# Edge passes of a graph network: row tiles in a ring, a resident table of node blocks, and edge sums in two column halves

## The reference

```
def gatv2_layer(x, src, dst, Wl, Wr, att, bias, n_nodes, heads):
    xl = (x @ Wl).reshape(N, heads, Dh)
    xr = (x @ Wr).reshape(N, heads, Dh)
    e = leaky_relu(xl[src] + xr[dst], 0.2)
    logits = einsum('ehd,hd->eh', e, att)
    m = segment_max(logits, dst)
    a = exp(logits - m[dst])
    alpha = a / segment_sum(a, dst)[dst]
    out = segment_sum(alpha[:, :, None] * xl[src], dst)
    return out.mean(axis=1) + bias

h = relu(gatv2_layer(x, ..., heads=8)); h = gatv2_layer(h, ..., heads=4)   # with a loop edge per node
x = layernorm(x + h)
agg = segment_sum(x[src], dst)
x = layernorm(x + dense3(x + agg))
```

## Time and profile before

| | us |
|---|---|
| median of 3 runs | 4044.32 |
| lowest, highest | 4044.29, 4049.66 |
| span of the profiled execution | 4048.7 |

### The profile page before, as it was taken

How to read it: one execution, slowest core, us unless ns; L and a number is a source line. 1 busy time by engine, 2 the same in 40 slices (tenths; PEclk the granted TensorE clock), 3 DMA queues, 4 the chain that set the end, 5 groups by cost and what they waited for, 6 DMA issues and landing times. The chain is left out here.

```text
span 4048.7 us, 76266 instructions
## 1 busy us (share of the span) xinstructions
PE 3293.6 (81%) x24199; PEld 2204.4 (54%) x24199; DVE 2807.3 (69%) x6887; ACT 1717.6 (42%) x3696; POOL 2796.9 (69%) x2157
## 2 busy tenths in 40 slices
PE   0399999999999999996339977777777777568986
PEld 0246666666666666674226655554455555346763
DVE  3558888888888888886537755565555555579972
ACT  3254444444444444432215433333333333147861
POOL 4488888888777777505678888888888885537630
PEclk9999999999999999986669988888888888569997
DMA  2233343343333333323114433333333332211210
GB/s 58 51 65 80 86 88 86 86 89 85 80 87 86 86 85 88 75 54 83 48 36 79 91 74 67 68 69 67 67 68 73 69 68 48 52 26 40 44 34 28
DMA packets 607173, 274.68 MB, mean 68 GB/s; under 512 B 445801, under 2 KB 568077, under 8 KB 606260
## 3 DMA queue, kind: packets, MB, share of 16 engines
q1 hardware_dynamic: 261848, 102.14, 11.7%
q0 software_dynamic: 107328, 77.78, 11.1%
q10 hardware_dynamic: 237600, 89.88, 9.1%
HBM read 161.25 MB, written 105.94 MB: 66 GB/s over the span
## 5 line engine op out<-in xcount | busy, mean ns | idle before, releaser
L901 PE MATMUL L_e_ps_z<-L_e_xT,L_w_abs 128*128 128x500 f32 x2700 | 1501.4, 642 | 0.0
L826 POOL DMA_INDIRECT L_e_xs<-in_x_dram,src_idx x880 | 1193.1, 1356 | 335.4 <-issue 261.4
L826 POOL DMA_INDIRECT L_e_xs<-x_d,src_idx x820 | 1079.7, 1317 | 253.3 <-issue 249.8
L952 PEld LDWEIGHTS L_e_ps_v<-L_e_xs,L_e_p 125*128 125x128 f32 x5400 | 860.0, 204 | 628.3 <-issue 569.6
L996 ACT ACTIVATE L_e_rl<-L_e_ps_z 128x500 f32<-128x500 f32 x1350 | 793.0, 587 | 883.0 <-PE L_e_ps_z L901 883.0
L952 PE MATMUL L_e_ps_v<-L_e_xs,L_e_p 125*128 125x65 f32 x5400 | 796.2, 274 | 11.1 <-DVE L_e_acc L1180 9.4
L1180 DVE SCALAR_TENSOR_TENSOR L_e_acc<-L_e_acc,L_e_row,L_e_ps_v 128x130 f32<-128x130 f32 (+1 forms) x1440 | 448.5, 311 | 424.1 <-PE L_e_ps_v L952 281.4
L888 PE MATMUL L_e_ps_x<-ident,L_e_xs 125*64 125x125 f32 x1800 | 288.7, 285 | 310.7 <-DMA L_e_xs<-x_d,src_idx 251.8
L989 ACT ACTIVATE L_e_xT<-L_e_ps_x 128x500 f32<-128x500 f32 x450 | 264.3, 587 | 619.3 <-PE L_e_ps_x L891 590.4
L901 PEld LDWEIGHTS L_e_ps_z<-L_e_xT,L_w_abs 128*128 128x128 f32 x2700 | 427.4, 198 | 77.8 <-issue 24.3
L1163 DVE TENSOR_TENSOR L_e_p<-L_e_ohc,L_e_ae 125x640 f32<-125x640 f32 x540 | 427.1, 818 | 0.0
(11 more groups left out here) (304 smaller groups left out, 3620.2 us busy)
## 6 DMA issues: line engine op xcount, KB each, us to landing
L_v_d<-L_e_acc ACTq DMA_DIRECT2D x225, 260.0 KB
L_e_dlb<-dloc_d SPq DMA_DIRECT2D x90, 468.8 KB, 4.9
L_v_d<-L_e_acc ACTq DMA_DIRECT2D x225, 130.0 KB
L_e_xw<-x_d SPq DMA_DIRECT2D x1800, 12.0 KB
L_e_xs<-in_x_dram,src_idx POOLq DMA_INDIRECT x900
L_e_xs<-x_d,src_idx POOLq DMA_INDIRECT x900
L_e_lim<-limits_d SPq DMA_DIRECT2D x180, 39.1 KB
L_max_d<-L_e_me SPq DMA_DIRECT2D x45, 78.1 KB
```

Of the source, the lines that this page charges most:

```text
L826: pool.indirect_dma_start(xs[c.slot(XR)][:, n, 0:D], None, lay.x_rows, bass.IndirectOffsetOnAxis(k.src_idx[:, u:u + 1], 0)).then_inc(gath[ ...
L901: pe.matmul(ps_z[part % ZR][:, 0:QT], lay.w_abs[:, part * 128:(part + 1) * 128], xT[q][:], start=True, stop=True).then_inc(s["z_ready"], 1)
L952: ins = pe.matmul(ps_v[u // 2 % 2][:, u % 2 * VX + v * XW:u % 2 * VX + (v + 1) * XW], p[st % 3][:, u % NQ, v, :, :].rearrange("e n h -> e ...
```

## The change

It does four things.

1. **Tiles instead of units are gathered.** `src_tile` holds the row numbers of the 800 tiles. GpSimd gathers tiles in fetches of 16 (`TF`) into a ring of 64 tiles (`TR`), `e_tiles`. For a fetch it waits for a count (`copied`) that says that the chunks which use the old tiles have been copied, and it signals a fetch that has landed (`fetched_to`) when four gathers of the next are issued. For each chunk SP waits for the fetch that it needs and then copies its 20 tiles from the ring into `xs` with 20 SBUF-to-SBUF DMAs at places from registers (`load_rows`). `xs` is a ring of 6 chunks in both layers. In layer 1 two fetches are made in the block before the pass and one chunk is served there; in layer 2 two fetches in each of the two blocks, and chunks 0, 1, 2 served.
2. **The windows are resident.** All 98 window blocks are loaded once a layer (`lay.xw`, 96 rows, 64 zero columns ahead of them). `turn` takes 128 columns of it from a place in a register as the stationary side, so that the product fills all of `ps_x`; the transposes come after it and overwrite the upper half. The places are loaded on TensorE at the end of the step before (`window_blocks`).
3. **Each sum is two products of 64 columns**, the one to PSUM partitions 0 to 63, the other to 64 to 127. The sums of a quad stand together, after `turn`, and the projection parts together behind them.
4. **Setup**: 2 of the 9 source gathers by unit remain (the neighbour sum uses them), tiles are turned with 8 transposes, and three lists of units (place of the window, place in the ring, fetch needed) are stored in `unit_d`. In layer 1 the rings of `dlb` and of the limits have two slots instead of three, and one `p` buffer lies in memory of a later tensor. The copy of `dlb` for a chunk is still queued on SP behind the loads for that chunk.

```
-AHEAD = (1, 4)
-EARLY = 35
+TR = 64
+TF = 16
+NF = G // TF
+RF = TR // TF
+XR = 6
+LR = 8
+SERVED = (1, 3)
+FETCHED = (2, 4)
...
+def counts(eng, name, places):
+    regs = [eng.alloc_register(f"{name}{n}") for n in range(places.shape[1])]
+    eng.load(regs, places)
+    return [(eng.snap(r, donate=True, min_val=0, max_val=63) & 63) + 1 for r in regs]
+
+def fetch_tiles(k, pool, lay, f0, f1):
+    for f in range(f0, f1):
+        if f >= RF:
+            if (f - RF) % 16 == 0:
+                copies = counts(pool, f"{lay.nm}reuse{f}_", k.reuse[0:1, f - RF:min(f + 16, f1) - RF])
+            pool.wait_ge(lay.copied, copies[(f - RF) % 16])
+            pool.sem_inc(lay.freed, 1)
+        for i in range(TF):
+            g = f * TF + i
+            pool.indirect_dma_start(lay.tiles[:, g % TR * D:(g % TR + 1) * D], None, lay.x_rows,
+                                    bass.IndirectOffsetOnAxis(k.src_tile[:, g:g + 1], 0)).then_inc(lay.gath[f % RF], 16)
+            if i == 3 and f > f0:
+                tiles_there(pool, lay, f - 1)
+    tiles_there(pool, lay, f1 - 1)
+
+def tiles_there(pool, lay, f):
+    pool.wait_ge(lay.gath[f % RF], 16 * TF * (f // RF + 1))
+    pool.sem_inc(lay.fetched_to, 1)
+
+def listed(eng, lay, c, row, start, step, top):
+    regs = [eng.alloc_register(f"{lay.nm}{row}_{c.number}_{n}") for n in range(start, CU, step)]
+    eng.load(regs, lay.lists[c.slot(LR)][0:1, row, start:CU:step])
+    return [eng.snap(r, donate=True, min_val=0, max_val=top) for r in regs]
+
+def rows_there(sp, lay, c):
+    sp.wait_ge(lay.ld_r[c.slot(XR)], c.uses(XR) * 16 * CU)
+    sp.sem_inc(lay.copied, 1)
+
+def load_rows(k, sp, lay, c):
+    places = listed(sp, lay, c, 1, 0, 1, (TR - 1) * D)
+    sp.wait_ge(lay.fetched_to, counts(sp, f"{lay.nm}need{c.number}_", lay.lists[c.slot(LR)][0:1, 2, CU - 1:CU])[0])
+    for n, at in enumerate(places):
+        sp.dma_start(lay.xs[c.slot(XR)][:, n, 0:D], lay.tiles[:, bass.ds(at, D)]).then_inc(lay.ld_r[c.slot(XR)], 16)
+
+def serve(k, sp, lay, c):
+    sp.wait_ge(lay.ld_w[c.slot(2)], c.uses(2) * 16)
+    sp.sem_inc(lay.listed, 1)
+    if c.after(1):
+        rows_there(sp, lay, c.back(1))
+    load_rows(k, sp, lay, c)
...
 # SP in the pass
-                        if c.after(1):
-                            sp.wait_ge(ld_w[c.slot(2)], c.uses(2) * 16)
-                            load_windows(k, sp, lay, c)
+                        if c.after(lay.served):
+                            if c.after(XR):
+                                sp.wait_ge(s["v_ready"], c.val(CU, CU * (1 - XR)))
+                            serve(k, sp, lay, c)
+                        if c.after(SLACK):
+                            sp.wait_ge(s["oht_ready"], c.val(1, 1 - SLACK))
                         sp.dma_start(dlb[r][:], ...
...
 # TensorE, turn
                     for j in range(Q):
                         n = j * NQ + q
-                        pe.transpose(ps[0:D, j * T:(j + 1) * T], xs[r][:, n, 0:D], k.ident[0:T, 0:T])
+                        pe.matmul(ps[:, j * T:(j + 1) * T], xw[:, bass.ds(blocks[j], 128)],
+                                  oht[c.slot(2)][:, n * T:(n + 1) * T], start=True, stop=True)
                     for j in range(Q):
                         n = j * NQ + q
-                        ins = pe.matmul(ps[D:128, j * T:(j + 1) * T], xw[c.slot(3)][:, n, :],
-                                        oht[c.slot(2)][:, n * T:(n + 1) * T], start=True, stop=True)
+                        ins = pe.transpose(ps[0:D, j * T:(j + 1) * T], xs[r][:, n, 0:D], k.ident[0:T, 0:T])
...
 # TensorE, sums and the order of a step
                     for v in range(HV):
-                        ins = pe.matmul(ps_v[u // 2 % 2][:, u % 2 * VX + v * XW:u % 2 * VX + (v + 1) * XW],
-                                        p[st % 3][:, u % NQ, v, :, :].rearrange("e n h -> e (n h)"),
-                                        xs[c.slot(XR)][:, u, :], start=True, stop=True)
+                        for half in range(2):
+                            ins = pe.matmul(ps_v[u // 2 % 2][64 * half:64 * half + 64, u % 2 * VX + v * XW:u % 2 * VX + (v + 1) * XW],
+                                            p[st % 3][:, u % NQ, v, WN // 2 * half:WN // 2 * (half + 1), :].rearrange("e n h -> e (n h)"),
+                                            xs[c.slot(XR)][:, u, :], start=True, stop=True)
...
-                    for part in range(4):
-                        if part % (4 // C) == 0 and (c.after(1) or q >= 1) and zc.there():
-                            project(zc, zq, part // (4 // C))
-                        if c.after(3) and bc.there():
-                            sums(bc, bq, part)
+                    if c.after(3) and bc.there():
+                        for n in range(Q):
+                            sums(bc, bq, n)
+                    if (c.after(1) or q >= 1) and zc.there():
+                        for part in range(C):
+                            project(zc, zq, part)
                     if (c.after(1) or q >= 3) and rc.there():
                         reduce(rc, rq)
...
+                    nc_, nq = lag(c, q, -1)
+                    if nc_.there():
+                        blocks[:] = window_blocks(nc_, nq)
```

More of the change, by code:

```diff
@@ L305, in _ @@
                 xs.wait()
+                l3.wait()
             @block.gpsimd
@@ L820, in _ @@
             def _(pool):
-                for c in map(fixed, range(lay.ahead, NCH)):
-                    if c.after(XR):
-                        pool.wait_ge(s["v_ready"], c.val(CU, CU * (1 - XR)))
-                    for n in range(CU):
-                        u = c.val(CU, n)
-                        pool.indirect_dma_start(xs[c.slot(XR)][:, n, 0:D], None, lay.x_rows,
-                                                bass.IndirectOffsetOnAxis(k.src_idx[:, u:u + 1], 0)).then_inc(gath[c.slot(XR)], 16)
+                fetch_tiles(k, pool, lay, lay.fetched, NF)
                 for r in range(2):
@@ L1495, in _ @@
                              allow_slow_non_contiguous=True).then_inc(s["load"], 16)
+                for c in range(1, lay.served):
+                    serve(k, sp, lay, fixed(c))
                 sp.wait_ge(s["load"], 48)
```

203 lines of the change are left out of this document (124 added, 79 removed).

## The result

The changed kernel takes 4070.5 us (median of three executions, 4062.7 to 4073.8) against 4047.0 for the kernel before, run beside it: 1.0056 of it, 95% interval 1.0039 to 1.0072. A fourth execution took 4387.2 us at a mean granted clock of 0.73, where the others had 0.91, and is left out of the comparison. The kernel is slower by half a per cent, where 3855 was forecast.

A forecast was written before the change was run, and what follows sets the result against it. TensorE was taken to bound layer 1 and GpSimd's gathers layer 2. Layer 1 with setup -88 and layer 2 -104 summed to -192 from 4044.3: 3852, say 3855 us, own range 3800 to 3900, overall 3750 to 3985.

The forecast's parts named there:

- Registers on TensorE: Four window places loaded per step, 0.8 to 1.84 us, taken as covered by the last projection and reduction, 1.4 us.
- Rival D: TensorE stalls in register loads each step, gap over 0.9 us before the first window product: 4215 us, chance 0.08.
- Sums and projections: Layer 1 step: sums 1.16 us, projections 3.6, whole step 6.11 instead of 6.74; chunk taken at 33.1.
- layer 1, the rest: Layer 1 behind its first four chunks: 39 chunks at 2.3 us less each, 90 us less.
- Rival B: Layer 1 sums: strips do not overlap, a pair takes 0.11 us, only the gathers' gain remains: 3976 us, chance 0.15.
- the change of kind: Layer 1 sums: 0.2 us a step for the change-over and first load.
- Rival C: Layer 1 falls to VectorE's 29.6 and GpSimd's 29.4 us, stopping at about 30.3 a chunk: 3744 us, chance 0.13.
- Chunk 5 begins some 5 us late: Start of layer 1: chunks 1 to 5 come at GpSimd's pace, the one-hot queued behind copies holding each iteration before.
- Copies: SP's 20 copies a chunk with their register loads: 11.5 us, bounds 8 and 16.
- E: Copies become the bound in both layers, 42 us a chunk; slower than before from 1.7 us a copy: 4787, chance 0.03.
- Layer 2: Gathers end 134 us earlier (736 in 1192 us, 5 for waits), some 30 us longer behind the last: -104.

The follow-up runs named there:

- f2: Changed kernel with one window place loaded behind each projection part (two in layer 2), not four behind the reduction: 3938.8 us, 0.9731 of the kernel before.
- f1: Changed kernel with window blocks at constant places, no registers loaded on TensorE, output not the reference's: 3938.2 us, 0.9739 of the kernel before.
- h1: Changed kernel with its one load of four places moved ahead of the reduction, behind the last projection: 3958.0 us, 0.9783 of the kernel before.
- f7: Changed kernel with one place loaded behind each part and the one-hot source issued before the rows are served: 3915.1 us, 0.9684 of the kernel before.
- i2: Changed kernel with one place a part, source first and halves in both layers, run again: 3917.0 us, 0.9685 of the kernel before.
- i1: Changed kernel with one place a part, source first, halves in layer 1 alone, full-width sums in layer 2: 3877.0 us, 0.9586 of the kernel before.
- g5: Kernel before with each sum as two 64-column products, in the old order (each part, then its unit's sums): 4138.2 us, 1.0195 of the kernel before.
- g4: Kernel before with a step's full-width sums together, then its projection parts together: 4104.3 us, 1.0105 of the kernel before.
- h3: Kernel before with both halves and grouping of the sums, nothing else of the change: 4018.2 us, 0.9936 of the kernel before.
- h4: Changed kernel with one place a part and source first, but full-width grouped sums in both layers: 3944.8 us, 0.9757 of the kernel before.

## Why the prediction was wrong

**Registers on TensorE: the step that failed.** The prediction put the load of four places at nothing ("I take it as covered in layer 1 and in layer 2"), because the array would still have the last projection and the reduction, 1.4 us, to do while the sequencer was at the load. It hadn't: the registers cost 141 us, 0.54 us a step of layer 1. The prediction had read from the earlier trace rows that the sequencer runs ahead of the array, and that is so, but not far enough. In the step shown the sequencer was at the wait ahead of the reduction at 1147.48, when the last projection began. The load began at 1148.54, when four of the reduction's sixteen weight loads had gone in; in all 55 steps of 500 to 1500 us with no transposes behind the reduction it is after exactly the fourth. That left 0.6 us of array work against 1.0 of load and 0.26 of waits and register instructions behind it. My reading is that what the array holds ready is limited, here to twelve weight loads and their products; no run varied that.

The duration was estimated well (0.99 to 1.94, median 1.17, for 0.8 to 1.84). Rival D named the mechanism and had 0.08. Its sign was a gap of over 0.9 us before the first window product of each step. On the array the gap was 0.64 in the step shown, 0.46 on average, and over 0.9 in 3 steps of 139, so by that sign alone D would have been turned down. The 0.54 comes from three terms: the window products begin 0.58 later behind the work before them than in f2, they follow one another 0.21 more slowly as a quad, and the 0.25 that f2's sums wait for VectorE falls away. 0.54 in the 220 or so steps is 119 us, beside 111 missed in the table. f1, f2 and h1 show it, h1 that position is most of it.

The register load isn't all of the miss. From the changed kernel run again (4079) to 3855 there are 224 us: 141 are the registers (f1, f2), 24 the place of the one-hot source (f2 to f7), 40 the halves in layer 2 (i2 to i1, 38 from f7's 3915), and some 22 are left.

**Sums and projections: right.** 1.08 for 1.16, 3.66 for 3.6, step 6.05 for 6.11, chunk 33.3 for 33.1. Once the load is covered and the source is first (f7), the row "layer 1, the rest" of the table has -85 for the -90 forecast. Rival B, a pair at 0.11, is out: within a quad a pair follows another by 0.058. But I took the change of kind at 0.2 a step without asking whether strips can be loaded under a projection. The change groups the quad, so that came out right by its order and not by my reason (g5). Rival C's VectorE wasn't met at 29.6 but felt at 33.3: 1.0 a chunk.

**The first chunks.** "Chunk 5 begins some 5 us late" was 39 at chunk 4, 15 before the first relu and 24 behind it: chunk 0 waits for the next chunk's whole fetch and its copies, not for the copies alone. f7 took 13 to 14 of it off chunk 0, and 24 off the total.

**Copies.** 20 with their load took 16.7 + 1.7 us instead of 11.5, beyond the bound of 16: a copy's issue takes SP 0.71 us (median of 1800) where a window load's took 0.32. Three such blocks stand on the path ahead of the passes, one before layer 1 and two before layer 2, 7 us more each; the table misses 8 and 9 there. In the passes a copy takes 0.83 us of SP, half of the 1.7 from which E was slower than before, so E is out. The cause of the longer issue isn't known.

**Layer 2.** The 736 gathers take 1215 us from first to last, 1.65 each, where 1192 and 5 for the waits were forecast: 18 us. Another 29 lie at the end. The last relu comes 30.8 us behind the start of the last gather in the kernel before, 89.8 in the changed one, so +59 where +30 was forecast. SP's rows there (after GpSimd's last gather) show two sets of copies and not one, since the last two chunks both wait for the last fetch:

```profile
3367.36 1.21 POOL L599 DMA_INDIRECT L_e_tiles<-x_d,src_tile  x1 [0.31 <-issue]
```

```profile
3371.23 16.68 SPq L635 DMA_DIRECT2D L_e_xs<-L_e_tiles  x20
...
3393.30 16.64 SPq L635 DMA_DIRECT2D L_e_xs<-L_e_tiles  x20
```

With full-width sums and the source first (i1) the layer gives 101 us, as was forecast, but by luck: its gathers run at 1.607, faster than the 1.62 forecast, and its end is still 13 longer. That the sums of a layer in which TensorE isn't the bound could cost its gathers anything was in none of the steps.

Had the load been behind the projection parts, the source first and the halves in layer 1 alone, 3855 would have been missed by 22 us.

## To carry to other kernels

An instruction that an engine's sequencer executes itself is covered only if the sequencer gets there early. See in the trace when it gets there, and how much work of the array is left then. Put such loads where the sequencer stands and waits while the array works (here at the relu waits between projections), ahead of the work that is to hide them and not behind it. Narrow weights pay in a row of their own kind, not between full-width products. An operation made faster in a stage that another engine bounds isn't free: measure it per stage, and keep it where it gains.

## What the runs showed of the hardware

- A load of registers from SBUF on TensorE: one value 0.31 us (median of 1800), four strided ones 1.07 to 1.17 (medians of h1 and of the changed kernel), on SP twenty in a row 1.74, one 0.27. The Trainium skill (Runtime: NRT & Kernel Launch, instruction fetch mechanics) has about 200 ns a register for loads from HBM; for one to four values from SBUF 0.27 to 0.31 a value was seen here, for twenty in a row 0.09.
- TensorE's sequencer ran ahead of the array by a bounded amount: with the sixteen weight loads of a reduction just ahead of a register load, the register load began when the fourth of them had gone in (55 steps of 55 in the changed kernel).
- GpSimd's gathers in layer 2 (2500 to 3200 us, traces without pauses): 1.29 to 1.31 us beside full-width sums; beside two-strip sums 1.31 to 1.32 without the ring and 1.34 to 1.38 with it. In layer 1 they take 1.355 before, 1.34 and 1.36 in g4 and g5, and 1.38 to 1.43 in h3 and all versions with the ring, whatever the width (h4 1.434). What they share isn't shown by these runs.
- On one chip, programs with the ring of tiles took 15 to 17% longer than the kernel before, by pauses of ScalarE of up to 15 us at no fixed place, all of them while GpSimd was gathering; the kernel before took 4061 to 4088 there instead of 4045 to 4047. The cause stays open.
